# Normalizing finished tiles before the last sums, and a gate that takes Silu from x

## The reference

```python
def _layernorm(x, axis=-1, eps=1e-05):
    m = jnp.mean(x, axis=axis, keepdims=True)
    v = jnp.var(x, axis=axis, keepdims=True)
    return (x - m) / jnp.sqrt(v + eps)
...
x = x + jnp.tanh(g_xattn[0]) * _L0_xattn_ref(_layernorm(x, axis=-1), ctx_1024, ...)
x = x + jnp.tanh(g_ffn[0]) * _L0_ffn_ref(_layernorm(x, axis=-1), ...)
x = x + jnp.tanh(g_xattn[1]) * _L1_xattn_ref(ctx_1024, _layernorm(x, axis=-1), ...)
x = x + jnp.tanh(g_ffn[1]) * _L1_ffn_ref(_layernorm(x, axis=-1), ...)
x = x + jnp.tanh(g_xattn[2]) * _L2_xattn_ref(_layernorm(x, axis=-1), ctx_1024, ...)
x = x + jnp.tanh(g_ffn[2]) * _L2_ffn_ref(_layernorm(x, axis=-1), ...)
x = x + jnp.tanh(g_xattn[3]) * _L3_xattn_ref(ctx_1024, _layernorm(x, axis=-1), ...)
x = x + jnp.tanh(g_ffn[3]) * _L3_ffn_ref(_layernorm(x, axis=-1), ...)
```

```python
y = jnp.moveaxis(ys, 0, -1)
y = y + D[None, :, None] * u
y = y * jax.nn.silu(z)
```

## Time and profile before

| | us |
|---|---|
| median of 3 runs | 1278.52 |
| lowest, highest | 1273.51, 1278.64 |
| the profiled execution | 1275.05 |
| its span, first to last instruction | 1273.3 |
| PE busy in it | 1068.6 (84%) |
| DVE busy | 822.8 (65%) |
| ACT busy | 677.3 (53%) |
| POOL busy | 675.0 (53%) |
| mean granted clock of TensorE | 0.914 of 2.4 GHz |

### The profile page before, as it was taken

How to read it: one execution, slowest core, us unless ns; L and a number is a source line. 1 busy time by engine, 2 the same in 40 slices (tenths; PEclk the granted TensorE clock), 3 DMA queues, 4 the chain that set the end, 5 groups by cost and what they waited for, 6 DMA issues and landing times.

```text
span 1273.3 us, 18231 instructions
## 1 busy us (share of the span) xinstructions
PE 1068.6 (84%) x5382; PEld 834.3 (66%) x5382; DVE 822.8 (65%) x1515; ACT 677.3 (53%) x1718; POOL 675.0 (53%) x452
## 2 busy tenths in 40 slices
PE   6576788778747978999999999798999746999993
PEld 3455577656514766888888888665555444888883
DVE  3892799689779751666666565859998683333332
ACT  4466555444554235778787777467663124333331
POOL 2105888888823232444454545429997103786653
PEclk8888799899958998999999999989999857999997
DMA  6494999897440013011101110305542993877655
GB/s 189 140 199 120 238 287 292 214 278 175 55 131 1 1 51 92 16 59 51 54 18 55 54 50 2 104 1 154 153 141 55 268 270 101 182 166 130 104 73 132
DMA packets 153171, 154.49 MB, mean 121 GB/s; under 512 B 35188, under 2 KB 140396, under 8 KB 153076
## 3 DMA queue, kind: packets, MB, share of 16 engines
q1 hardware_dynamic: 129092, 123.04, 33.5%
q0 software_dynamic: 22896, 29.24, 14.2%
q10 hardware_dynamic: 1088, 1.05, 0.2%
HBM read 123.11 MB, written 30.18 MB: 120 GB/s over the span
## 4 chain that ended last, share of the span: by engine, by line
PE 54%; POOL 16%; DVE 12%; issue 8%; DMA 5%; ACT 3%; SPq 0%; POOLq 0%; DVEq 0%; ACTq 0%
PE bank L2496 8%; POOL f_sums L1023 6%; PE bank L1600 4%; PE bank L1696 4%; PE bank L1685 4%; PE bank L1663 4%; POOL arena L1009 4%; PE bank L1589 2%; DMA f_sums<-arena,put 2%; PE bank L1618 2%; PE bank L1674 2%; PE bank L2125 2%; PE bank L2514 2%; PE bank L2516 2%; POOL arena L560 2%
## 5 line engine op out<-in xcount | busy, mean ns | idle before, releaser
L540 DVE TENSOR_TENSOR_SCAN arena<-arena 128x1024 f32<-128x1024 f32 x64 | 155.3, 2427 | 19.7 <-issue 12.2
L1023 POOL DMA_INDIRECT f_sums<-arena,put x64 | 124.0, 1937 | 22.8 <-issue 17.7
L560 POOL TENSOR_TENSOR arena<-arena 128x1024 f32<-128x1024 f32 x32 | 82.4, 2574 | 88.8 <-DVE arena L540 88.8
L2393 POOL DMA_INDIRECT e_sums<-ctxT,put x63 | 98.7, 1567 | 57.0 <-DVE ctxT L2695 40.1
L1009 POOL DMA_INDIRECT arena<-y_rows,slots x64 | 82.8, 1294 | 67.2 <-DVEq L1224 45.9
L2496 PE MATMUL bank<-arena,ssm_y 128*128 x504 | 108.4, 359 | 0.4 <-issue 0.4
L518 ACT ACTIVATE arena<-arena,ssm_A 128x255 f32<-128x255 f32 x256 | 108.0, 498 | 0.2
L2125 PE MATMUL bank<-yT,arena 128*128 128x512 f32 (+1 forms) x224 | 103.2, 605 | 3.3 <-ACT arena L2056 3.3
L570 PE MATMUL bank<-arena,ident 128*128 128x256 f32 x256 | 72.2, 431 | 33.9 <-DVE arena L560 30.5
L2689 DVE TENSOR_TENSOR ssm_y<-ssm_y,bank 128x256 f32<-128x256 f32 x63 | 26.6, 422 | 114.2 <-ACT ssm_y L2571 68.1
L529 DVE TENSOR_TENSOR arena<-arena 128x1024 f32<-128x1024 f32 x64 | 94.3, 1473 | 0.0
(11 more groups left out here) (343 smaller groups left out, 2722.8 us busy)
## 6 DMA issues: line engine op xcount, KB each, us to landing
arena<-bc_rows SPq DMA_DIRECT2D x64, 512.0 KB
y<-e_sorted SPq DMA_DIRECT2D x62, 128.0 KB
arena<-in_L_ffn_w_gate_dram SPq DMA_DIRECT2D x16, 256.0 KB
arena<-in_L_ffn_w_up_dram SPq DMA_DIRECT2D x16, 256.0 KB
arena<-in_L_ffn_w_down_dram SPq DMA_DIRECT2D x16, 256.0 KB
x<-in_L_ffn_w_gate_dram SPq DMA_DIRECT2D x16, 256.0 KB
y<-in_L_ffn_w_up_dram SPq DMA_DIRECT2D x16, 256.0 KB
yT<-in_L_ffn_w_down_dram SPq DMA_DIRECT2D x16, 256.0 KB
```

Of the source, the lines that this page charges most:

```text
L540: nc.vector.tensor_tensor_scan(ssm_h[:, j % 2, :], ssm_decay[:, j % 2, :], ssm_in, 0.0, ALU.mult, ALU.add).then_inc(s_ssm_h, 1)
L560: ops.tensor_tensor(ssm_hC_buf[:, j % 2, :], ssm_h[:, j % 2, :], ssm_C[:, g % 2, :], ALU.mult).then_inc(s_ssm_hC, 1)
L1023: nc.gpsimd.indirect_dma_start(out=f0_sums[m % SUMS], out_offset=bass.IndirectOffsetOnAxis(ap=put[:, m:m + 1], axis=0), in_=f0_ye[:, n % R ...
L2393: nc.gpsimd.indirect_dma_start(out=e_sums[t % 2], out_offset=bass.IndirectOffsetOnAxis(ap=put[:, t:t + 1], axis=0), in_=e_ye[:, t % 4, :], ...
```

## The change

`norm_dve` gets a list of pairs. Norm 4 is split: pairs 0 to 2 are written before `add(7)` of layer 1's ffn, pair 3 stays at the head of `x_dve`; PE gets a wait for all sums of layer 1 ahead of norm 4's transposes, whose PSUM banks the sums read. Norm 5 is split too: pairs 0 and 1 between the copy and the last sum of layer 2's mixer, pairs 2 and 3 where all stood. In the gates, norms 2 and 6 no longer write y: ACT computes Silu(x * rstd + shift) for each tile (L621), with shift = -mean * rstd made by DVE for each pair in a new small tile z_shift (L627). In layer 1 three of the four shifts follow the statistics of the next batch, and the fourth comes behind the first product; layer 3 has three ahead of the first product and one behind it. On ACT the gate of layer 1 moves ahead of `ssm_lin_act`.

```diff
--- before.py
+++ after.py
@@ -195,8 +195,8 @@
                 nc.vector.tensor_scalar(var_eps[:, 2 * j:2 * j + 2], moments[:, 2 * j:2 * j + 2, 1], EPS, None,
                                         ALU.add).then_inc(s_var, 1)
 
-        def norm_dve(dve, k):
-            for j in range(NT // 2):
+        def norm_dve(dve, k, pairs=range(NT // 2)):
+            for j in pairs:
                 dve.wait_ge(s_rstd, NT // 2 * k + j + 1)
                 for i in (2 * j, 2 * j + 1):
                     nc.vector.tensor_scalar(y[:, i, :], x[:, i, :], moments[:, i, 0:1], rstd[:, i:i + 1],
@@ -612,21 +612,32 @@
         s_z_t = sem("s_z_t")
         s_z_x = sem("s_z_x")
 
+        z_shift = sb("z_shift", [P, NT])
+
         def gated_act(act, m, k):
             for b in range(B):
                 act.wait_ge(s_y, NT * k + TPB * (b + 1))
-                nc.scalar.activation(z_gate[:, TPB * b:TPB * (b + 1), :], y[:, TPB * b:TPB * (b + 1), :],
-                                     ACT.Silu).then_inc(s_z_silu, 1)
+                for i in range(TPB * b, TPB * (b + 1)):
+                    last = nc.scalar.activation(z_gate[:, i, :], x[:, i, :], ACT.Silu, bias=z_shift[:, i:i + 1], scale=rstd[:, i:i + 1])
+                last.then_inc(s_z_silu, 1)
+
+        def gated_shift(dve, k, b):
+            dve.wait_ge(s_rstd, NT // 2 * k + b + 1)
+            tiles = slice(TPB * b, TPB * (b + 1))
+            nc.vector.scalar_tensor_tensor(out=z_shift[:, tiles], in0=moments[:, tiles, 0], scalar=-1.0, in1=rstd[:, tiles],
+                                           op0=ALU.mult, op1=ALU.mult).then_inc(s_y, TPB)
 
         def gated_dve(dve, m, k):
 
             if m:
-                norm_dve(dve, k)
+                for b in range(B - 1):
+                    gated_shift(dve, k, b)
                 dve.wait_ge(s_ssm_red_y, B * HC)
             else:
-                norm_dve(dve, k)
                 dve.wait_ge(s_ssm_y, B * HC)
             for b in range(B + 1):
+                if b == 1:
+                    gated_shift(dve, k, B - 1)
                 if b < B:
                     dve.wait_ge(s_z_silu, m * B + b + 1)
                     rows = z_gate[:, TPB * b:TPB * (b + 1), :]
@@ -1260,6 +1271,8 @@
                 dve_link(nc.vector.tensor_tensor(rows, rows, more[:, 0, :], ALU.add))
                 nc.vector.tensor_tensor(rows, rows, more[:, 1, :], ALU.add).then_inc(s_f0_x, 1)
                 norm_stats(dve, range(TPB * b, TPB * (b + 1)), s_f0_x, b + 1)
+                if b:
+                    gated_shift(dve, 2, b - 1)
 
         A1, R1, K1 = 64, 16, 4
         AR = A1 * R1
@@ -1445,6 +1458,8 @@
                     choose(i + 1)
                 if i == 0:
                     ssm_dt_dve(dve, 1, 1)
+                if i == NT - 1:
+                    norm_dve(dve, 4, range(B - 1))
                 add(i)
 
         def l1_pool(pool):
@@ -1712,6 +1727,7 @@
 
             pe.wait_ge(s_l1_mv, NT)
             keys(0, 0, (4, 5), 0)
+            pe.wait_ge(s_l1_x, NT)
             norm_pe(pe, 4, 3)
             pe.wait_ge(s_yT, 4 * NT // 2)
             queries(0, 0, 0, 0)
@@ -1830,7 +1846,7 @@
 
         def x_dve(dve):
             V = nc.vector
-            norm_dve(dve, 4)
+            norm_dve(dve, 4, (B - 1,))
             dve.wait_ge(s_x_g, 48)
             V.tensor_tensor(x_gqk[:, 0:1], x_gqk[:, 0:1], x_gqk[:, 1:2], ALU.mult).then_inc(s_x_gqk, 1)
 
@@ -1909,6 +1925,7 @@
             add(end - 2, B - 2)
             norm_stats(dve, range(2 * TPB, 3 * TPB), s_x_add, end - 1)
             mixed_copy(end - 1, B - 1)
+            norm_dve(dve, 5, range(B - 2))
             add(end - 1, B - 1)
             norm_stats(dve, range(3 * TPB, 4 * TPB), s_x_add, end)
 
@@ -2183,7 +2200,7 @@
         def g_dve(dve):
             V = nc.vector
             dve.wait_ge(s_x_add, H * B)
-            norm_dve(dve, 5)
+            norm_dve(dve, 5, range(B - 2, B))
             wait(dve, s_g_logit, 1)
             logits = bank[6][:, 0:NT * E2].rearrange("p (i e) -> p i e", i=NT)
             dve_link(V.tensor_reduce(g_top[:, :], logits, AX_X, ALU.max))
@@ -2759,8 +2776,8 @@
             f0_more_act(act)
             ssm_u_act(act, 1)
             ssm_dbl_act(act, 1)
+            gated_act(act, 0, 2)
             ssm_lin_act(act, 1)
-            gated_act(act, 0, 2)
             for h in range(2):
                 ssm_dt_act(act, 1, 0, h)
             l1_act(act)
```

## The result

Five runs of each kernel, in turn on one chip: the changed kernel took 1270.9 us in the median (1268.32 to 1271.55), the kernel before 1275.84 (1273.51 to 1278.64). The measured ratio is 0.9949, with a 95% interval of 0.9934 to 0.9964 (the quotient of the two medians, 0.9961, lies inside it). The prediction was 1272.4 in a range of 1265 to 1279. So the gain is 0.5 to 0.7% by the two ratios, and 0.4 to 0.9% with their intervals.

The account below looks back on a forecast made before the run. Layers run one after another, bounded at four places by the engine waited for (DVE, ACT or PE). Gains 2.05 + 0 + 2.9 + 1.2 = 6.15 us took the median 1278.52 to 1272.4, range 1265 to 1279.

Parts of the forecast that it names:

- Layer 1's gate, 2.05: Layer 1's gate: norms leave DVE's path, transposes start right behind PE's L440, and the sum comes 2.05 us earlier.
- the 2.3 that the prediction gives for DVE alone: Layer 1's gate: the gain if DVE, not PE's L440, set when the transposes start, 2.3 us.
- ACT 0.5 late, "covered: two microseconds of room": Behind layer 1's gate: ACT's later work runs 0.5 us late, covered by two microseconds between squares and DVE's choice.
- End of layer 1, 0: End of layer 1: norms move into DVE's idle time, but ACT's squares of the keys hold the copies; gain 0.
- at most 0.4 if ACT were not the one: End of layer 1: upper bound of the gain if ACT did not hold the copies, 0.4 us.
- End of layer 2, 2.9: End of layer 2's mixer: four norms fill DVE's idle time, PE goes on without pause, experts start 2.9 us earlier.
- pause at pair 2: End of layer 2's mixer: PE never waits for pair 2; a pause there would show the prediction wrong.
- Layer 3's gate, 1.2: Layer 3's gate: three shifts replace the norms, ACT's Silu sets the first product, 1.2 us earlier (1.0 to 1.4).
- (a): Rival: TensorE's clock rises early at the end of layer 2's mixer, 2 to 4 us less, 1268.4 to 1270.4; chance 0.17.
- (b): Rival: a gain is given back, by the clock at three places or norms waiting for POOL, 3 us, 1275.4; chance 0.22.
- (c): Rival: DVE and POOL fall into another step, four more slow L560 cost 7.9 us, 1280.3; chance 0.07.
- (d): Rival: the change doesn't do what it says, as when the gate's first product still waits, 1277 to 1279; chance 0.04.

Follow-up runs that it names:

- e7: The changed kernel itself, unmodified, timed again on another chip; ratio 0.9929 to the kernel before.
- e1: The kernel before with only norm 5 split at the end of layer 2's mixer; ratio 0.9968 to the kernel before.
- e3: The kernel before with only the norm 4 split at the end of layer 1 and PE's wait; ratio 1.0 to the kernel before.
- e5: The kernel before with the new tile z_shift set aside in SBUF but never used; ratio 0.9985 to the kernel before.
- e8: The changed kernel with two of ACT's four L454 moved between the Silus of batches 1 and 2 in layer 1; ratio 0.9959 to the kernel before.
- e10: The changed kernel with idle PE transposes in layer 1, 19 at the gate and norm 3, 24 before tile 0's P transposes; ratio 0.9957 to the kernel before.
- e12: The changed kernel with ACT's copies to yT ahead of its squares of the keys at layer 1's end; median 1265.36 us, ratio 0.9908 to the kernel before.
- e11: The changed kernel with 18 and 40 idle PE transposes ahead of the first two expert blocks of layer 3; ratio 0.9962 to the kernel before.

## Why the prediction was right, step by step

**Layer 1's gate, 2.05.** Right in size (369.37 + 1.16 is 370.53, not 370.55, so by its own terms the gain is 2.09). It is 2.19 in the pair of profiles and 2.23 as a mean over all (15.53 in four with the old gate, 13.30 in ten with the new). PE's L440 was the limit, as said, in the profile after: L659 starts at 371.61, in the end of L440. That is not a property of the kernel. The same program in e7:

```profile
364.78 3.69 PE L440 MATMUL bank<-x_dbl,dtT 8*128 8x512 f32 x8 [0.67 <-ACT x_dbl L448]
370.52 1.11 PE L659 MATMUL bank<-ident,y 128*128 128x128 f32 x4 [2.05 <-DVE y L644]
```

There L440 ran at full clock, and the transposes waited 2.05 for DVE's product. In four of the ten kernels with the new gate L440 took 5.1 to 5.5 and was the limit (gate 13.2 to 13.7), in six it took 3.7 and DVE was (12.7 to 13.4). The means are 13.5 and 13.2, so it matters by 0.3, and the 2.3 that the prediction gives for DVE alone is what the six show against 15.5. A shift takes 0.15 to 0.16, and in the gate of layer 1 the next instruction starts 0.08 to 0.11 behind its start, inside the bounds. A pair of Silus takes 1.09, priced 1.1. The Trainium skill ("ScalarE: Activation LUTs", section "What ACT_TABLE_LOAD costs") gives 1.08 by the prediction's estimate from it; the trace's 1.09 agrees.

**ACT 0.5 late, "covered: two microseconds of room".** Here a step failed. The delay was nearly right (0.7 to 0.8 between the gate's sum and the first vectors: 14.35 before, 15.1 after), but the room was not there. It was read from the earlier trace rows, from one execution, in which the squares came 3.74 behind the start of the vectors. In e1, e3 and e5, with the same instructions there, they came 5.6 to 6.1 behind, and the choice followed 0.1 behind their end. The room was the clock having risen early in the profile that I read: 0.8 ahead of the vectors, where it rose 3.8 to 4.7 behind their start in those three. Tile 0's products come 0.56 later against the gate's sum with the new gates (35.60, the mean of eight without e8 and e10, against 35.04 in the four), so gate 1 is worth 1.7, not 2.05. The same 1.7 is left at layer 1's last addition.

**End of layer 1, 0.** Right, and for the reason given: the squares of the keys hold the copies (474.42 here, 474.43 before). What I wrote beside it, "at most 0.4 if ACT were not the one", was far too small; e12 took ACT out of the way and got 2.3 at once and, in its one profile, 3.8 to 4.0 by the experts. I had bounded what the norms could bring and not asked what else stood in that queue and who read it.

**End of layer 2, 2.9.** Right mechanism, 0.3 too small: 3.2 (9.83 against 13.01). In e7 and e11 the clock fell only behind the first transposes and the experts started 8.28 behind the sum, but the sum had come 1.7 later there, so that the stretch *layer 2* is the same (362.74 and 362.75). I let the transposes start at the modelled end of L1696; they start 0.2 ahead of it, 1.12 behind its start. In the profile after PE did not pause at pair 2, and the sum was no later. In e7, with the clock still at full there, PE did pause, 0.72 for DVE's norms of pair 2, which the prediction had named as a sign of being wrong; the stretch was no longer for it.

**Layer 3's gate, 1.2.** Right: it is 1.17, and ACT's Silu is what the first product waits for, as said.

**What the sum did not hold.** The tail, 1.4: 245.6 with a long gate 3, 244.2 with a short one (means of five and nine). The prediction took it that 1.2 there passes on as 1.2.

The mended sum is 2.2 - 0.6 + 0 + 3.2 + 1.2 + 1.4 = 7.4; the column *all* gives 8.2 (915.1 in the three without any part that acts, 906.9 in the three of the changed kernel). Predicted were 6.15, and 4.9 were measured between the two medians of the first pair (6.5 by the ratio), 9 to 10 in e7's group. In the profiles layer 0 alone spreads by 10.8, more than everything that the change does; that it also makes the difference between the timed medians is likely and not shown, since those runs have no trace. So the mechanisms at four places were right in the main, two terms were missed (0.6 lost, 1.4 won), and that 1270.9 lies as near 1272.4 as it does is in part luck: the median before, too, was 2.7 below the one from which the prediction starts.

**Rivals.** (a), an early rise at the mixer's end: no. The granted clock was 0.50 from 822 on, 0.70 from 835 to 836 and full behind that, so it rose 3.3 behind the experts' start; before it was full at 840, 3.4 behind it. In e7 and e11, where it had fallen later, it rose 2.8 behind that start. (b), a gain given back to the clock: in part, 0.56 at tile 0, and more than balanced by the tail, which moved the other way by the same cause. The moment of the change differs between executions of one program: in the profile after the clock fell at 821.9, 0.6 ahead of the mixer's last sum, in e7 at 826.9, 4.2 behind it, and the same sixteen vectors took 9.12 and 8.57. That agrees with what the prediction took from the Trainium skill ("TensorE: Matmul & The Clock Gate", section "What's actually happening"). (c), L560 slower on POOL: no. The same view of that line after (ns min/median/max, first and last start) reads

```profile
L560 POOL TENSOR_TENSOR arena<-arena x16: 2336/2352/4339, 847.4 to 971.8; 128x1024 f32<-128x1024 f32 x16
```

which is the earlier trace rows moved by 4.4. (d), that the change doesn't do what it says: no, by the timelines above.

## What to carry to other kernels

Room that one profile shows in front of an engine is only as good as the clock in that execution: before a delay is written off as covered, look how long the work in front of it took in a second one. When a transfer or a copy is ready and still waits, look at what its engine does in between and when that is read: here eight small squares that ended at 474.4, and whose keys PE first reads at 489.6, were worth more (3.8 to 4.0 in one profile) than the norms moved at the end of layer 2's mixer (3.2). And a change of a few microseconds is better measured by its own stretch in several profiles than by whole times, when another part of the kernel spreads by ten.
